# Four pairs of sampled products added by accumulating transfers, and the next image's sums on ScalarE, in a deformable convolution kernel

## The chip, the cores and the metric

One core of a Trainium2 chip runs the whole program. The time is that of the device, in microseconds, from one launch. Each engine runs its own queue in order: TensorE (PE), VectorE (DVE), ScalarE (ACT), GpSimd (POOL) and SyncE (SP). They meet only at semaphores. POOL and SP also issue transfers, which the core's 16 DMA engines carry out; POOL's can add to what lies at their destination.

## What is computed

An image batch (8, 64, 64, 256) goes through two layers, each `x = x + conv(groupnorm(x))`. The change touches only the first, a deformable convolution with 32 groups of 8 channels and 9 taps:

```
xdw    = depthwise3x3(x) + dw_b
om     = xdw @ om_w + om_b          # per group: 9 offsets (x, y), 9 masks
value  = x @ vp_w + vp_b
out[g] = sum over 9 taps of mask * bilinear(value[g], at tap + offset)
x      = x + out @ op_w
```

Group norm needs mean and variance of each group of 8 channels over the 64 x 64 pixels of an image. The second layer is a binarised 3x3 convolution, which the change leaves alone.

## The kernel before

Offsets here stay under one pixel, so the nine taps with bilinear weights fall on a fixed 5 x 5 window of shifts. `layer0` therefore makes 25 weight planes (`wsum`), multiplies the values by each, shifted, and sums the 25 products.

Image n is worked in four steps j = 0 to 3, so 32 steps s = 4n + j in all. In a step 128 partitions are 4 row blocks x 32 groups, with 4 rows x 64 columns = 256 pixels and 8 channels each. A step runs over nine taps k = 0 to 8, and work of neighbouring steps is interleaved:

- For each tap PE makes offsets and mask (`ps_om`, L746), two taps ahead. ACT turns them into hat functions and mask (`hat`, `msk`, L583 to L597). DVE multiplies mask by the hats (`mwy`, L923) and then makes nine products (L937), called P0 to P8 below. The products that start a plane go to `wsum`, the rest to `prod`. Those in `prod` are added to `wsum` by DVE for k = 4, 5, 8 (L965) and by an accumulating transfer of POOL for k = 1, 2, 3, 6, 7 (`SENT_TAPS`, L474); k = 7 takes two transfers. P(k+1) waits until the sum of tap k has landed (L943), since `prod` is used again.
- DVE multiplies shift uv, called M0 to M24, `pv` <- `val` x plane (L984), into one of four buffers, `(j + uv) % 4`, of 128 x 2048 float32 = 1 MiB. It waits for the sum of shift uv - 4 (`add_done`, L981).
- PE adds each product into PSUM by 16 transposing matmuls against the identity (`add`, L791). `SAMPLES_AT` says at which k which shifts are made: M0 to M12 at k = 4 to 8, M13 to M24 at k = 0 to 3 of the next step. PE's order is the same: one shift between the offsets of a tap, the others at the tap's end.
- At k = 4 ACT copies the finished sum into `acc`, PE turns it back (`turn_back`, L759) and ACT keeps `acc_t`; at k = 5, 6 PE projects it. POOL then adds x to `xres` by four accumulating transfers (L464), and DVE takes their statistics (`statistics`, L994) a step later, at k = 0.
- SP loads windows and the rows for the depthwise product. A load is issued when PE has used up what lay there, mostly at k = 0 to 3.

The next image's group norm needs its statistics early. For j = 0 and 1 of each image but the last, POOL loads half of one channel half (128 x 2048) into `acc` once `turn_back` has read it (L457, waiting for "back3" at k = 4), and the other half into `acc_t` once the projection is done. DVE takes `bn_stats` of `acc` at k = 7 (`sums_ahead`, L883) and of `acc_t` at k = 0 of the next step, four instructions each time. At j = 2 DVE aggregates them at k = 0 (`scales_ahead`, L896), PE averages over groups, and the scales are ready at k = 6.

Of the kernel before, what the change touches and what calls it, by code (L numbers as in the profile page):

```python
# [12 lines left out]
P = 128  # L13
H = W = 64
HW = H * W
# [21 lines left out]
SAMPLED = 4  # L37
SENT_TAPS = (1, 2, 3, 6, 7)
# [190 lines left out]
def layer0(nc, x, zeros, w_dram, x2, consts, tables, mv2, reach, NI):  # L229


    with ExitStack() as ctx:
# [26 lines left out]
        bs1 = sb("bs1", [P, CH, HW // 512, 6])  # L259
# [32 lines left out]
        pv_full, add_done, add_out = sem("pv_full"), sem("add_done"), sem("add_out")  # L292
        xres_added, stats2 = sem("xres_added"), sem("stats2")
        gn_kept = sem("gn_kept")
        x_ahead = [sem("x_ahead0"), sem("x_ahead1")]
        sums_made, gx_step = sem("sums_made"), sem("gx_step")
        gx_root = sem("gx_root")
        GX_STEPS = 11
# [54 lines left out]
        with nc.Block() as block:  # L353
# [97 lines left out]
            def _(pool):  # L451
# [24 lines left out]

                for n in range(NI):
                    for j in range(STEPS):
                        for k in SENT_TAPS:
                            if k == 6 and j < CH and n < NI - 1:  # L480
                                load_ahead(n, j, 0, "back3")
                            add_products(n, j, k)
                        if j < CH and n < NI - 1:
                            load_ahead(n, j, 1, "project3")
                        if (n, j) != (0, 0):
                            add_residual(*previous(n, j), unit(n, j, "project3", NI) + 1)

# [13 lines left out]
            def _(act):  # L501
# [98 lines left out]
                def summed(s):  # L600

                    act.wait_ge(add_done, SHIFTS * (s + 1))
# [21 lines left out]
                def keep_mean(n, j, i):  # L624

                    act.wait_ge(bg_full, unit(n, j, f"mean{i}", NI) + 2)
                    nc.scalar.activation(gmean[:, i, :], ps_bg[:, bank(n, j, f"mean{i}", NI), 0:CH], ACT.Copy)\
                        .then_inc(bg_free, 2)

# [20 lines left out]
                def step(n, j, first, last):  # L650
# [8 lines left out]
                    for k in range(TAPS):  # L659
                        if k in MEANS_AT and has_means(n, j, NI):  # L660
                            keep_mean(n, j, MEANS_AT.index(k))
                        if k == ROOT_AT and has_means(n, j, NI):
                            act.wait_ge(gx_step, GX_STEPS * n + 9)
# [26 lines left out]
                        if k == 6 and not last and j1 == 0:  # L690
                            normalise(n1, j1, 1)
                        if k == 8 and more:
# [10 lines left out]
            def _(pe):  # L703
# [72 lines left out]
                def group_mean(n, j, i, src):  # L776


                    pe.wait_ge(gx_step, GX_STEPS * n + (4, 8)[i])
# [4 lines left out]
                def add(s, j, uv):  # L784
                    pe.wait_ge(pv_full, SHIFTS * s + uv + 1)
                    if uv == 0:
                        at_least(pe, add_out, s)
                    for tb in range(TB):
                        for c in range(GC):

                            mm = nc.tensor.matmul(ps_add[:, tb, c, :], pv[:, (j + uv) % PBUF, c, P * tb:P * tb + P],  # L791
                                                  consts["ident"][:, :], start=uv == 0 and c % 4 == 0,
                                                  stop=uv == SHIFTS - 1, is_transpose=True, skip_group_check=True)
# [11 lines left out]
                def step(n, j, first, last):  # L805
# [3 lines left out]
                    def add_next(k, i):  # L809
                        if k < SAMPLED and not first:  # L810
                            add(s - 1, j - 1, SAMPLES_AT[k][i])
                        elif k >= SAMPLED and i < len(SAMPLES_AT[k]):
                            add(s, j, SAMPLES_AT[k][i])
# [4 lines left out]
                    for k in range(TAPS):  # L818
# [9 lines left out]
                        add_next(k, 0)  # L828
# [15 lines left out]
                        add_next(k, 1)  # L844
                        add_next(k, 2)
# [4 lines left out]
                for k in range(SAMPLED):  # L850
                    for uv in SAMPLES_AT[k]:
# [8 lines left out]
            def _(dve):  # L860
# [18 lines left out]
                def sums_ahead(n, j, half):  # L879

                    dve.wait_ge(x_ahead[half], 16 * (CH * n + j + 1))
                    for i in range(HW // 1024):
                        last = nc.vector.bn_stats(bs1[:, j, HW // 1024 * half + i, :], ahead[half][:, 512 * i:512 * i + 512])  # L883
                    last.then_inc(sums_made, 1)

                def scales_ahead(n, j, part):
# [6 lines left out]
                    if part == 0:  # L893

                        for h in range(CH):
                            nc.vector.bn_aggr(mv1[:, h, :], bs1[:, h, :, :]).then_inc(gx_step, 1)  # L896
                        dve.wait_ge(gx_step, GX_STEPS * n + 1 + CH)
                        after(3, nc.vector.tensor_copy(mean1[:, :], mv1[:, :, 0]))
                    elif part == 1:

                        dve.wait_ge(bg_free, unit(n, j, "mean0", NI) + 2)
                        after(4, nc.vector.tensor_tensor(mean1[:, :], mean1[:, :], gm, ALU.subtract))
                        after(5, nc.vector.tensor_tensor(mean1[:, :], mean1[:, :], mean1[:, :], ALU.mult))
                        after(6, nc.vector.tensor_tensor(var1[:, :], mv1[:, :, 1], mean1[:, :], ALU.add))
                        nc.vector.nop().then_inc(gx_step, 1)
                    elif part == 2:
                        dve.wait_ge(bg_free, unit(n, j, "mean1", NI) + 2)
                        after(8, nc.vector.tensor_scalar(var1[:, :], gmean[:, 1, :], EPS, None, ALU.add))
                    else:
# [3 lines left out]
                        after(9, nc.vector.reciprocal(gx[:, 0, :], var1[:, :]))  # L913
                        after(10, nc.vector.scalar_tensor_tensor(out=gx[:, 1, :], in0=gm, scalar=-1.0,
                                                                 in1=gx[:, 0, :], op0=ALU.mult, op1=ALU.mult))

                        after(11, nc.vector.tensor_scalar(tables[:, 0:2, bass.ds((n + 1) * CH, CH)], gx[:, :, :], 1.0, None,
# [50 lines left out]
                def multiply(n, j, uv):  # L968
# [11 lines left out]
                    if not isinstance(s, int) or s > 0 or uv >= PBUF:  # L980
                        dve.wait_ge(add_done, SHIFTS * s + uv - PBUF + 1)  # L981
# [33 lines left out]
                def step(n, j, first, last):  # L1015
# [7 lines left out]
                    for k in range(TAPS):  # L1023
# [13 lines left out]
                        if k == AHEAD_AT and j < CH and has_next(n):  # L1037
                            sums_ahead(n, j, 0)
                        if k == 0 and j in (1, 2) and has_next(n):
                            sums_ahead(n, j - 1, 1)  # L1040
# [834 lines left out]
```

## Time and profile before

| | us |
|---|---|
| median of 3 runs | 3881.9 |
| lowest, highest | 3876.69, 3891.0 |
| profiled execution, its own time | 3880.13 |
| its span, first to last instruction | 3878.3 |
| first layer's 31 step periods, 175.84 to 3368.84 us | 3193.0 |

The profile has a page with busy times of each engine, groups of instructions by source line with the idle time ahead of them and what ended it, the waits, the transfers, and a timeline. A step is recognised by the one `TENSOR_REDUCE` of L1010 at k = 8; the last table line is the distance between the first and the last of the 32. PE and DVE are both above 95% busy in it, while ACT is at 62%. The DMA engines are busy 52% of it, and that load comes in bursts.

### The profile page before, as it was taken

To read this page: it belongs to the slowest core of one execution; us is meant where nothing else is said; L and a number is where in the kernel's file an instruction comes from. 1 tells how busy PE (TensorE), PEld (TensorE's weight loads), DVE (VectorE), ACT (ScalarE), POOL (GpSimd) and SP (SyncE) were. 2 spreads that over 40 slices of the span, in tenths; PEclk is the share of its full clock that TensorE was granted. 3 is DMA by queue.
4 is the path that set the end of the run, shared out by engine and by line. 5 is a ranking of instruction groups with operands and counts; after the bars stand their busy time and mean duration, and the time that the engine had idled before them with its cause. 6 is when DMAs were issued, how large, how long until landed. Compare 5 with 4: busy or idle time off the path is not lost. (4 is left out here: it accounts for less than half of the span.)

```text
span 3878.3 us, 90671 instructions
## 1 busy us (share of the span) xinstructions
PE 3634.4 (94%) x37696; PEld 2370.7 (61%) x37696; DVE 3511.8 (91%) x2757; ACT 2286.1 (59%) x4547; POOL 565.0 (15%) x412
## 2 busy tenths in 40 slices
PE   3799999999999999999999999999999999858998
PEld 1466666666666666666666666666666666623333
DVE  2799999999999999999999999989999999958776
ACT  3665666666556656666666666665566665325554
POOL 0011100111111111111110111111111111104444
PEclk9999999999999999999999999999999999979999
DMA  5454555556554455456545555555545544335563
GB/s 142 109 118 100 116 112 121 111 109 121 131 121 100 96 124 122 101 110 132 129 98 115 117 124 119 109 113 126 117 98 107 105 103 94 60 147 201 214 215 146
DMA packets 319939, 470.35 MB, mean 121 GB/s; under 512 B 37244, under 2 KB 242684, under 8 KB 313736
## 3 DMA queue, kind: packets, MB, share of 16 engines
q0 software_dynamic: 94080, 196.11, 28.2%
q1 hardware_dynamic: 224872, 266.08, 23.0%
q8 instruction: 298, 4.88, 0.5%
q10 hardware_dynamic: 544, 2.10, 0.1%
q14 instruction: 145, 1.19, 0.1%
HBM read 262.53 MB, written 67.41 MB: 85 GB/s over the span
## 5 line engine op out<-in xcount | busy, mean ns | idle before, releaser
L984 DVE TENSOR_TENSOR pv<-val,wsum 128x2048 f32<-128x2048 f32 x800 | 1812.5, 2288 | 7.4 <-PE ps_add L791 7.4
L791 PEld LDWEIGHTS ps_add<-ident,pv 128*128 128x128 f32 x12800 | 1403.0, 142 | 350.0 <-issue 237.2
L791 PE MATMUL ps_add<-ident,pv 128*128 128x128 f32 x12800 | 1529.5, 276 | 65.4 <-DVE pv L984 57.1
L746 PE MATMUL ps_om<-xdw,omw 128*32 128x256 f32 x13824 | 872.0, 385 | 26.9 <-ACT hat L585 26.0
L937 DVE TENSOR_TENSOR prod<-hat,mwy 128x1536 f32<-128x1536 f32 (+1 forms) x384 | 526.5, 1399 | 96.5 <-DMA wsum<-prod 75.5
L474 POOL DMA_DIRECT2D wsum<-prod x192 | 226.0, 1254 | 2598.9 <-DVE wsum L937 2598.9
L583 ACT ACTIVATE hat<-ps_om,omb 128x256 f32<-128x256 f32 x576 | 276.1, 479 | 552.1 <-PE ps_om L746 506.8
L746 PEld LDWEIGHTS ps_om<-xdw,omw 128*32 128x32 f32 x13824 | 391.8, 110 | 328.6 <-issue 95.9
L587 ACT ACTIVATE msk<-ps_om,omb 128x256 f32<-128x256 f32 x288 | 137.1, 476 | 401.6 <-PE ps_om L746 399.4
L923 DVE TENSOR_TENSOR mwy<-hat,msk 128x768 f32<-128x768 f32 x288 | 275.0, 955 | 93.8 <-ACT hat L597 93.8
L718 PE MATMUL ps_bg<-tri,diag 128*32 128x512 f32 x3024 | 347.3, 593 | 0.0
L731 PE MATMUL ps_bg<-win,vpw 128*32 128x256 f32 x5120 | 304.2, 384 | 35.3 <-DMA ident<-in_ident_dram 27.1
L538 ACT ACTIVATE tri<-tri,gn_tri 96x1024 f32<-96x1024 f32 (+1 forms) x376 | 329.9, 951 | 8.7 <-ACT gn_tri L509 4.5
L585 ACT ACTIVATE hat<-ps_om,omb 128x256 f32<-128x256 f32 x576 | 281.4, 489 | 0.0
L584 ACT ACTIVATE hat<-ps_om,nomb 128x256 f32<-128x256 f32 x576 | 276.7, 480 | 0.0
L937 DVE TENSOR_TENSOR wsum<-hat,mwy 128x768 f32<-128x768 f32 (+2 forms) x288 | 257.9, 895 | 2.7 <-DVE pv L984 1.3
L731 PEld LDWEIGHTS ps_bg<-win,vpw 128*32 128x32 f32 x5120 | 167.3, 111 | 149.5 <-DMA ident<-in_ident_dram 27.1
L772 PE MATMUL ps_bg<-acc_t,opw 128*128 128x512 f32 x512 | 238.4, 606 | 1.8 <-ACT acc_t L612 0.7
L965 DVE TENSOR_TENSOR wsum<-wsum,prod 128x1536 f32<-128x1536 f32 x192 | 226.2, 1221 | 0.0
L1688 POOL TENSOR_TENSOR c_x<-c_x,c_res 128x1024 f32<-128x1024 f32 x64 | 170.4, 2666 | 340.5 <-ACT c_res L1572 340.5
L1641 PE MATMUL ps_p<-c_over,c_kw 128*128 128x512 bf16 x768 | 189.0, 396 | 18.8 <-ACT c_res L1566 18.8
L718 PEld LDWEIGHTS ps_bg<-tri,diag 128*32 128x32 f32 x3024 | 98.9, 111 | 176.0 <-issue 155.4
(120 smaller groups left out, 2607.8 us busy)
## 6 DMA issues: line engine op xcount, KB each, us to landing
wsum<-prod POOLq DMA_DIRECT2D x160, 768.0 KB, 7.0
tri<-in_x_dram SPq DMA_DIRECT2D x725, 128.0 KB, 2.9
win<-in_x_dram SPq DMA_DIRECT2D x148, 256.0 KB, 3.5
x<-xres SPq DMA_DIRECT2D x128, 256.0 KB, 5.2
xres<-in_x_dram POOLq DMA_DIRECT2D x124, 256.0 KB, 8.7
out_dram<-c_x SPq DMA_DIRECT2D x31, 1024.0 KB, 4.7
c_x<-x SPq DMA_DIRECT2D x30, 1024.0 KB, 5.4
c_box<-box_d SPq DMA_DIRECT2D x16, 1024.0 KB, 7.1
```

The lines of the kernel that those rows point to most:

```text
L538: last = nc.scalar.activation(v, v, ACT.Identity, bias=gn_tri[0:KROWS, j % 2, 2 * c + 1, h:h + 1], scale=gn_tri[0:KROWS, j % 2, 2 * c, h:h ...
L583: nc.scalar.activation(hat[:, par, a, 1, :], d, ACT.Abs, bias=b).then_inc(abs_done, 1)
L584: nc.scalar.activation(hat[:, par, a, 0, :], d, ACT.Relu, bias=nb, scale=-1.0)
L585: nc.scalar.activation(hat[:, par, a, 2, :], d, ACT.Relu, bias=b).then_inc(om_free, 1)
L718: mm = nc.tensor.matmul(out[:, :, :, o0:o1], diag[:, h, c, kx, :], src, start=kx == 1, stop=kx == 2)
L731: mm = nc.tensor.matmul(ps_bg[G * q:G * q + G, par, ci * TOK:(ci + 1) * TOK], vpw[:, h, 2 * cp + ci, :], win[:, h, q, :, :], start=h == 0, ...
L746: mm = nc.tensor.matmul(ps_om[G * q:G * q + G, (par + i) % 2, 0:TOK], omw[:, h, comp, :], xdw[:, j % 2, h, q, :], start=h == 0, stop=h == ...
L772: mm = nc.tensor.matmul(ps_bg[:, par, :], opw[:, h, P * oh:P * oh + P], acc_t[:, h, 512 * tb:512 * tb + 512], start=h == 0, stop=h == CH - 1)
L791: mm = nc.tensor.matmul(ps_add[:, tb, c, :], pv[:, (j + uv) % PBUF, c, P * tb:P * tb + P], consts["ident"][:, :], start=uv == 0 and c % 4 ...
L923: nc.vector.tensor_tensor(mwy[:, :, :], hat[:, par, 1, :, :], msk[:, par, :].unsqueeze(1).to_broadcast([P, 3, TOK]), ALU.mult)\
L937: return nc.vector.tensor_tensor(dst, hat[:, par, 0, c:d, :].unsqueeze(1).to_broadcast(shape), mwy[:, a:b, :].unsqueeze(2).to_broadcast(sh ...
L984: nc.vector.tensor_tensor(pv[:, (j + uv) % PBUF, :, :].rearrange("p c (r w) -> p c r w", w=W), val[:, :, SR * j + u:SR * j + u + SR, v:v + ...
```

## The change

Two things change.

**Pairs.** For (target <- source) 1 <- 0, 3 <- 2, 12 <- 11 and 15 <- 14, POOL issues a transfer that adds the source's product buffer, 1 MiB, into the target's (`add_pair`). PE adds the target alone, so 21 shifts. PE's wait for a target is for the transfer (`pair_added`). DVE's wait before it writes a buffer that held a source is for the transfer as well. PE's order becomes `ADDS_AT`.

**Sums.** `sums_ahead` moves from DVE to ACT. At k = 7, and at k = 0 of the next step, ACT subtracts a pivot (the half's first value) from the 2048 values in place and accumulates the sum, then squares them and accumulates again. `scales_ahead` makes mean and variance out of those sums by five small instructions in place of two `bn_aggr` and a copy. DVE's wait for `sums_made` at k = 0 of j = 2 stays.

```diff
+PAIRED = {1: 0, 3: 2, 12: 11, 15: 14}
+ADDS_AT = [(13, 12), (16, 15, 17, 18), (19, 20, 21), (22, 23, 24), (), (1,), (4, 3, 5, 6), (7, 8, 9), (10,)]
...
+                def add_pair(n, j, uv):
+
+                    s = STEPS * n + j
+                    pool.wait_ge(pv_full, SHIFTS * s + uv + 1)
+                    at_least(pool, pair_added, 16 * (len(PAIRS) * s + PAIRS.index(uv)))
+                    nc.gpsimd.dma_start(pv[:, (j + uv) % PBUF, :, :], pv[:, (j + PAIRED[uv]) % PBUF, :, :], accum_op=ALU.add)\
+                        .then_inc(pair_added, 16)
+
                 for n in range(NI):
                     for j in range(STEPS):
+                        if (n, j) != (0, 0):
+                            add_pair(*previous(n, j), 15)
                         for k in SENT_TAPS:
-                            if k == 6 and j < CH and n < NI - 1:
-                                load_ahead(n, j, 0, "back3")
+                            if k == 6:
+                                if j < CH and n < NI - 1:
+                                    load_ahead(n, j, 0, "back3")
+                                add_pair(n, j, 1)
+                                add_pair(n, j, 3)
                             add_products(n, j, k)
                         if j < CH and n < NI - 1:
                             load_ahead(n, j, 1, "project3")
                         if (n, j) != (0, 0):
                             add_residual(*previous(n, j), unit(n, j, "project3", NI) + 1)
+                        add_pair(n, j, 12)
+                add_pair(NI - 1, STEPS - 1, 15)
...
+                def sums_ahead(n, j, half):
+
+                    act.wait_ge(x_ahead[half], 16 * (CH * n + j + 1))
+                    v, i = ahead[half], 3 * (CH * n + j)
+                    if half == 0:
+                        nc.scalar.activation(pivot[:, j:j + 1], v[:, 0:1], ACT.Copy, scale=-1.0).then_inc(centred, 1)
+                        act.wait_ge(centred, i + 1)
+                    nc.scalar.activation(v, v, ACT.Identity, bias=pivot[:, j:j + 1],
+                                         accum_out=x_sums[:, half, j, 0:1]).then_inc(centred, 1)
+                    act.wait_ge(centred, i + 2 + half)
+                    nc.scalar.activation(v, v, ACT.Square, accum_out=x_sums[:, half, j, 1:2]).then_inc(sums_made, 1)
...
                 def add(s, j, uv):
-                    pe.wait_ge(pv_full, SHIFTS * s + uv + 1)
-                    if uv == 0:
+                    if uv in PAIRED:
+                        pe.wait_ge(pair_added, 16 * (len(PAIRS) * s + PAIRS.index(uv) + 1))
+                    else:
+                        pe.wait_ge(pv_full, SHIFTS * s + uv + 1)
+                    if uv == ADDED[0]:
                         at_least(pe, add_out, s)
...
-                    if not isinstance(s, int) or s > 0 or uv >= PBUF:
-                        dve.wait_ge(add_done, SHIFTS * s + uv - PBUF + 1)
+                    used, in_step = (uv - PBUF, s) if uv >= PBUF else (uv - PBUF + SHIFTS, s - 1)
+                    if used in PAIRED.values():
+                        dve.wait_ge(pair_added, 16 * (len(PAIRS) * in_step + list(PAIRED.values()).index(used) + 1))
+                    elif not isinstance(s, int) or in_step >= 0:
+                        dve.wait_ge(add_done, ADDS * in_step + ADDED.index(used) + 1)
```

POOL's queue, from the first product transfers of a step with j = 1 to the next step's, before: `wsum<-prod` are the transfers of L474 for k = 1, 2, 3, 6, 7, `xres` the residual.

```order
L474 DMA wsum<-prod 128x3x512 [waits wsum_added,prod_done] x2
L474 DMA wsum<-prod 128x2x768 [waits wsum_added,prod_done]
L457 DMA acc<-in_x_dram 128x2048 [waits bg_full]
L474 DMA wsum<-prod 128x2x768 [waits wsum_added,prod_done] x2
L474 DMA wsum<-prod 128x512
L457 DMA acc_t<-in_x_dram 128x2048 [waits bg_full]
L464 DMA xres<-in_x_dram 128x2x256 [waits bg_free]
L464 DMA xres<-in_x_dram 128x2x256 x3
```

Now, from the same place on, with the pairs 1, 3 and 12, 15 as `pv<-pv`:

```order
L481 DMA wsum<-prod 128x3x512 [waits wsum_added,prod_done] x2
L481 DMA wsum<-prod 128x2x768 [waits wsum_added,prod_done]
L464 DMA acc<-in_x_dram 128x2048 [waits bg_full]
L489 DMA pv<-pv 128x2048 [waits pair_added,pv_full] x2
L481 DMA wsum<-prod 128x2x768 [waits wsum_added,prod_done] x2
L481 DMA wsum<-prod 128x512
L464 DMA acc_t<-in_x_dram 128x2048 [waits bg_full]
L471 DMA xres<-in_x_dram 128x2x256 [waits bg_free]
L471 DMA xres<-in_x_dram 128x2x256 x3
L489 DMA pv<-pv 128x2048 [waits pair_added,pv_full] x2
```

Pairs 1 and 3 stand ahead of the product transfer of k = 6, pair 12 behind the residual and pair 15 ahead of the product transfer of k = 1, each with a wait for the pair before it.

DVE's queue at k = 6 of a step with j = 1, before: the end of P6, then M4, the mask, M5 and M6.

```order
L937 TENSOR_TENSOR wsum<-hat,mwy 128x768
L981 REGISTER_ALU [waits wsum_added]
L984 TENSOR_TENSOR pv<-val,wsum 128x2048 [waits add_done]
L922 REGISTER_ALU [waits prod_done]
L923 TENSOR_TENSOR mwy<-hat,msk 128x768 [waits hat_full]
L981 REGISTER_ALU [waits wsum_added]
L984 TENSOR_TENSOR pv<-val,wsum 128x2048 [waits add_done]
L981 REGISTER_ALU [waits wadd_done]
L984 TENSOR_TENSOR pv<-val,wsum 128x2048 [waits add_done]
```

Now:

```order
L974 TENSOR_TENSOR wsum<-hat,mwy 128x768
L1019 ISA [waits wsum_added]
L1024 TENSOR_TENSOR pv<-val,wsum 128x2048 [waits pair_added]
L959 REGISTER_ALU [waits prod_done]
L960 TENSOR_TENSOR mwy<-hat,msk 128x768 [waits hat_full]
L1021 ISA [waits wsum_added]
L1024 TENSOR_TENSOR pv<-val,wsum 128x2048 [waits add_done]
L1019 ISA [waits wadd_done]
L1024 TENSOR_TENSOR pv<-val,wsum 128x2048 [waits pair_added]
```

Nothing is moved here; M4 and M6 wait for the transfers of pairs 1 and 3 (`pair_added`) where they waited for PE.

ACT's queue at k = 0 and 1 of a step with j = 2, before: the end of the hats, the depthwise result, the group mean, the next hats.

```order
L597 ACTIVATE hat<-hat 128x2x256 [waits w0_done]
L555 ACTIVATE xdw<-ps_bg,dwb 128x512 [waits bg_full]
L627 ACTIVATE gmean<-ps_bg 128x2 [waits bg_full]
L583 ACTIVATE hat<-ps_om,omb 128x256 [waits om_full,prod_done]
L584 ACTIVATE hat<-ps_om,nomb 128x256
```

Now:

```order
L619 ACTIVATE hat<-hat 128x2x256 [waits w0_done]
L577 ACTIVATE xdw<-ps_bg,dwb 128x512 [waits bg_full]
L659 ACTIVATE acc_t,x_sums<-acc_t,pivot 128x2048 [waits x_ahead1]
L662 ACTIVATE acc_t,x_sums<-acc_t 128x2048 [waits centred]
L649 ACTIVATE gmean<-ps_bg 128x2 [waits bg_full]
L605 ACTIVATE hat<-ps_om,omb 128x256 [waits om_full,prod_done]
```

Two activations over 128 x 2048 stand between the depthwise result and the group mean.

## Rows read from the trace of the kernel before

**Rows 1.** Groups by line: shapes, count | busy us, mean ns | idle before, releasers.

```profile
L984 DVE TENSOR_TENSOR pv<-val,wsum 128x2048 f32<-128x2048 f32 x800 | 1812.5, 2288 | 7.4 <-PE ps_add L791 7.4
...
L791 PE MATMUL ps_add<-ident,pv 128*128 128x128 f32 x12800 | 1529.5, 276 | 65.4 <-DVE pv L984 57.1 <-ACT acc L604 7.8
...
L604 ACT ACTIVATE acc<-ps_add 128x1024 f32<-128x1024 f32 x64 | 62.1, 1022 | 67.3 <-PE ps_add L791 67.3
...
L883 DVE BATCH_NORM_STATS2 bs<-acc 128x6 f32<-128x512 f32 x56 | 34.6, 684 | 0.0
...
L883 DVE BATCH_NORM_STATS2 bs<-acc_t 128x6 f32<-128x512 f32 x56 | 34.5, 681 | 0.0
```

**Rows 2.** Window: us; PE, PEld, DVE, ACT, POOL busy; clock, DMA share, GB/s.

```profile
175.84:3368.84 3193.00, 3104.74 (x34384) 2127.15 (x34380) 3051.86 (x2274) 1968.04 (x4098) 386.01 (x336) 1.00 0.52 112
```

**Rows 3.** Waits of DVE in that window: us, times, longest us.

```profile
DVE prod L937 <- DMA wsum<-prod: 64.7, 62, 2.2
DVE mwy L923 <- ACT hat L597: 40.8, 32, 3.8
DVE prod L937 <- issue: 16.3, 12, 3.2
```

**Rows 4.** Three short windows, columns as in the long one above.

```profile
1032.00:1033.00 1.00, 0.19 (x1) 0.19 (x2) 1.00 (x2) 0.97 (x3) 0.14 (x1) 0.90 0.32 57
1033.00:1036.00 3.00, 3.00 (x15) 3.00 (x15) 3.00 (x3) 0.00 (x0) 0.00 (x0) 0.50 1.11 193
...
1103.00:1105.00 2.00, 2.00 (x26) 1.66 (x28) 2.00 (x4) 1.13 (x4) 0.11 (x1) 1.00 1.04 368
```

**Rows 5.** DMA issues, 1030.5 to 1040 us: KB each, us to landing.

```profile
wsum<-prod POOLq DMA_DIRECT2D x1, 768.0 KB, 6.5
```

**Rows 6.** DMA issues of the whole span, page part 6.

```profile
acc<-in_x_dram POOLq DMA_DIRECT2D x14, 1024.0 KB, 5.3
```

**Rows 7.** Timeline of POOL, start us, us.

```profile
1030.85 1.28 POOL L474 DMA_DIRECT2D wsum<-prod  x1 [30.89 <-DVE wsum L937]
...
1075.58 0.59 POOL L457 DMA_DIRECT2D acc<-in_x_dram  x1 [20.27 <-PE ps_bg L759]
```

**Rows 8.** Timeline of DVE, k = 8 to k = 2, two steps.

```profile
1013.24 2.56 DVE L937 TENSOR_TENSOR wsum<-hat,mwy 128x2304 f32<-128x2304 f32 x1
...
1018.79 4.49 DVE L984 TENSOR_TENSOR pv<-val,wsum 128x2048 f32<-128x2048 f32 x2
...
1027.94 1.75 DVE L937 TENSOR_TENSOR prod<-hat,mwy 128x1536 f32<-128x1536 f32 x1
...
1037.94 0.60 DVE L1001 BATCH_NORM_AGGREGATE mv_now<-bs 128x2 f32<-128x48 f32 x2
...
1127.06 2.47 DVE L883 BATCH_NORM_STATS2 bs<-acc_t 128x6 f32<-128x512 f32 x4
...
1208.60 2.36 DVE L937 TENSOR_TENSOR prod<-hat,mwy 128x1536 f32<-128x1536 f32 x2 [2.14 <-DMA wsum<-prod]
```

**Rows 9.** Timeline of DVE, k = 5 to k = 7 of one step.

```profile
1071.72 2.36 DVE L937 TENSOR_TENSOR prod<-hat,mwy 128x1536 f32<-128x1536 f32 x2
...
1081.87 1.76 DVE L937 TENSOR_TENSOR prod<-hat,mwy 128x1536 f32<-128x1536 f32 x1
...
1084.40 2.29 DVE L984 TENSOR_TENSOR pv<-val,wsum 128x2048 f32<-128x2048 f32 x1
...
1087.47 4.50 DVE L984 TENSOR_TENSOR pv<-val,wsum 128x2048 f32<-128x2048 f32 x2
...
1091.88 2.37 DVE L937 TENSOR_TENSOR prod<-hat,mwy 128x1536 f32<-128x1536 f32 x2
```

**Rows 10.** Timeline of ACT, k = 0 and 1 of step j = 2.

```profile
1128.77 0.69 ACT L555 ACTIVATE xdw<-ps_bg,dwb 128x512 f32<-128x512 f32 x1 [0.71 <-PE ps_bg L718]
1133.38 0.17 ACT L627 ACTIVATE gmean<-ps_bg 128x2 f32<-128x2 f32 x1 [3.91 <-PE ps_bg L781]
```

**Rows 11.** Timeline of SyncE's queue, loads for the depthwise product.

```profile
1025.37 17.61 SPq L381 DMA_DIRECT2D tri<-in_x_dram  x12
```

## What is predicted, and from what

> **What bounds the kernel now.** I read the groups by line first, for who costs what; then the busy times of the stretch from the end of step 0 to the end of step 31, 3193.0 us; then what VectorE waits for in it; and last the timelines of single steps, because the change acts there.
>
> In that stretch VectorE is busy 3051.9 us and TensorE 3104.7 [rows 2]. Neither alone sets the pace. VectorE is idle 141.1 us, made up of 64.7 + 16.3 = 81 us at the start of a P, which is the transfer of the tap before (the profile names no releaser for the second figure, but it stands at the same instruction), 40.8 us for ACT's hats, 7.4 us for PE's sums and small rests [rows 1, 3]. The hats are late where PE has fallen behind; they and the 7.4 us are what a lighter PE can give back. The 81 us are transfers, and no engine's load changes them. So a lighter PE is worth at most 48 us, and what VectorE sheds comes on top.
>
> **What is taken away.** PE: four shifts a step. One is 1529.5 / 12800 x 16 = 1.91 us [rows 1], so 7.6 us a step and 237 us over 31 steps. PE then has 2868 us of work in 3193. It is no bound any more, and of the 237 us only the 48 above can reach the end. VectorE: the 112 `bn_stats`, 34.6 + 34.5 = 69.1 us [rows 1]. The five small instructions for mean and variance take the place of two aggregations and a copy, 7 times; I set that even. Together 48 + 69 = **117 us to be gained**, if nothing new is waited for.
>
> **What a pair costs as a transfer.** No row shows one, so I build it from the nearest: the product transfer of 768 KB, also accumulating, between the same memories and from the same queue. Issued at 1030.85 [rows 7], it moves data from about 1032.7 on at 193 GB/s, with the 16 engines full (share 1.11) [rows 4], and lands 6.5 us after its issue [rows 5]. That is 1.7 us to start, 0.786 MB / 193 GB/s = 4.1 us to move and 0.7 us to land. POOL wakes 0.4 us after DVE has finished. A pair is 1.049 MB: 0.4 + 1.7 + 5.4 + 0.7 = **8.2 us** from DVE's last write to the release. The other end is the plain load of 1 MiB, 5.3 us [rows 6] at 368 GB/s [rows 4]. I take 193, since an accumulating transfer has to read two operands for one written and the row nearest in kind shows about half the plain rate.
>
> The Trainium skill ("DMA: Bandwidth & Descriptors", Anatomy of one DMA — SWDGE (gpsimd) path) fits such a transfer as 2.0 us plus bytes / 436e3. By it a pair would take 4.4 us, an estimate from that page, and 768 KB 3.8 us. The trace doesn't agree for accumulating transfers: it has 6.5 us for 768 KB [rows 5]. What a fast pair would give is a rival below.
>
> **Where the pairs meet VectorE.** All times are from the example step, as distances.
>
> Pair 12. M12 ends at 1013.24 and M15, which writes over source 11, would begin at 1018.79 + 2.20 = 1020.99 [rows 8]: 7.75 us for an 8.2 us transfer. Late by 0.45 us alone, by up to 3 if SyncE's window load falls on it. I take 0.7 x 31 = **22 us**.
>
> Pair 15. It is issued as M15 ends, and P1 follows after the statistics alone, so P1 ends 5.0 us after M15. The pair moves from 2.1 to 7.5, the product transfer of k = 1 behind it in the queue to 11.6, and it lands at 12.3. P2 wants it at 5.0 + 7.5 = 12.5: P1 to P2 is 10.0 us [rows 8], 2.5 of it P1. Nothing is lost alone, but SyncE issues twelve loads of 128 KB from 1025.37 on [rows 11], half of them onto the pair; their 0.8 MB at the mixed rate cost about 3 us, and the slack is 0.2. I take 2.5 us, of which some 0.5 is in the 81 us already: 2.0 x 24 = **48 us** for all steps but the seven below (bounds 0 and 4 us each).
>
> Pairs 1 and 3 and the product transfer of k = 6. From the end of M1 (1071.72 = 0) [rows 9]: pair 1 lands at 8.2. M3 ends at 10.15, pair 3 is issued at 10.55 and moves from 12.25 to 17.65. P6 ends at 12.7; its product transfer is behind pair 3, moves from 17.65 to 21.75 and lands at 22.45. P7 would begin at 20.16 [rows 9]. Late by 2.3 us, where it is on time now; 17 steps, 39 us.
> In the 14 steps with j < 2 the 1 MiB load of `acc` goes out first. Its issue is at 1075.58 = 3.9 [rows 7]; with PE one shift lighter ahead of it I put 3.0. It moves from 4.7 to 7.55, pair 1 to 12.95 and lands at 13.65. Pair 3 waits for that landing before it is issued, moves from 15.45 to 20.85, and the product transfer to 24.95, landing at 25.65. Late by 5.5 us, 77 us. Together **116 us** (bounds: 2.3 in all, 71; 7 and 3.5, 158). What stands behind these waits on VectorE is P7, M7 to M9 and with them PE's next shifts.
>
> **Where the sums go.** ACT does 1024 elements in 1.02 us [rows 1], so two passes over 2048 are about 4.1 us, 28 times, 115 us on an engine that is busy 1968 of 3193 [rows 2]. Between the depthwise result, which ends at 1129.46, and the group mean ACT sits idle 3.91 us now [rows 10]; that cover is used up. But VectorE waits for `sums_made` at k = 0 of j = 2. M15 ends there at 1127.06 [rows 8] and ACT would be done at 1129.46 + 4.1 = 1133.6: 6.5 us of a new wait, 7 times, **46 us**. Statistics and P1 are queued behind it. Pair 15 lands under this wait, which is why P2 costs nothing in these steps. If ACT came to it sooner, it would be some 4 us (30 us).
>
> At k = 7 the sums have been covering something too. P8 waits for two product transfers; in a step without sums it waits 2.14 us [rows 8], and this kind of wait is 1.6 to 2.1 us in each of the seven steps that show it. With the sums away the steps j = 0 and 1 show it, and with PE no longer late the steps j = 3 too: 1.9 x 24 = **46 us**.
>
> **The sum.** New waits 22 + 48 + 116 + 46 + 46 = 278 us, against 117 gained: 161 us slower. From the profiled execution's 3880.1 us (span 3878.3; the median of the runs is 3881.9) that gives 4041 us. With the bounds of the terms, 14 + 0 + 71 + 30 + 46 = 161 at the low end, it would be 3924; at the high end 93 + 96 + 158 + 60 + 60 = 467, or 4230.
>
> **The rivals.**
> *Fast pairs.* The pairs move at the plain 368 GB/s. Then pair 12 lands in time, pair 3 moves from 12.25 to 15.1, and the product transfer lands at 19.9, before P7's 20.16. What is left of the new waits is 46 + 46 and some 10, or 102, against 117: 3865 us, no difference. For it speaks that a pair lies in 8 KB rows, as the plain load does, and the product transfer in shorter ones; against it the two operands read, which the length of a row doesn't change.
> *Fast pairs and hidden sums.* The same, and ACT gets to its sums before VectorE waits for them, since the lighter PE feeds it sooner: 56 against 117, or 3819 us, faster. This is the case the page's 4.4 us would lead to. Its turning point is where a pair takes less than 7.75 us from write to release, and the sums are done by 1127 in the example.
> *Half of it.* Rates as I have them, but the loads keep out of the way and the sums wait is short: 3900 to 3930.
> *TensorE's clock.* After 2.13 us of idleness PE was granted 0.90 and then 0.50 of its speed for three microseconds, the 1.2 GHz level [rows 4], and 16 matmuls of L791 took 3.6 us there where they take 1.9 otherwise. A PE that pauses at five or six places a step meets that each time. It has 325 us of slack, but if two such delays of 1.6 us a step reach VectorE through the hats, that is 100 us more: 4140 us.
>
> **How the numbers follow.** The forecast with its own spread, 3930 to 4120, 62 in 100. TensorE's clock or more collisions, above 4120, 13. Half of it, 6. Fast pairs alone, 8. Fast pairs and hidden sums, or something else that leaves the gain, 11. A measurement of this kernel can tell 0.5%, about 19 us. Below 3862 I put 0.13, between 3862 and 3901 0.09, and above 0.78. The range leaves out the fast cases and the far end: 3865 to 4160.
>
> **What would show it.** Right: VectorE's waits at the start of P7 grow from almost none to over 2 us a step, twice that where j < 2; the wait ahead of M15 is short but in each step; one long wait for ACT per image, at k = 0 of j = 2; PE's busy time is down by 245 us with much more idle time; the stretch of 31 steps is about 3354 us. The pairs take 7.8 us from issue to landing. Wrong: pairs that land in 5 to 6 us (fast pairs); no wait ahead of the statistics of j = 2; hats that VectorE waits for, which would mean that PE or ACT is the bound.

## The result and the profile after

| | before | after |
|---|---|---|
| median of 4 runs, us | 3883.2 | 4106.7 |
| lowest, highest | 3876.7, 3891.0 | 4097.3, 4113.8 |
| ratio, with its 95% interval | | 1.0573 [1.0544, 1.0602] |
| span of the profiled execution | 3878.3 | 4095.5 |
| first layer's 31 step periods | 3193.0 | 3401.8 |

The change costs 223.5 us. Forecast were 161 (4041 us; the range was 3865 to 4160). The first layer's 31 periods hold 208.8 of it. Their window row answers to [rows 2]: PE, PEld, DVE, ACT, POOL busy, granted clock, DMA share, GB/s.

```profile
177.38:3579.22 3401.84, 2984.67 (x32412) 1985.44 (x32404) 2992.83 (x2180) 2076.11 (x4221) 496.69 (x460) 0.95 0.69 143
```

PE has 120 us less to do, VectorE 59 us less, ACT 108 more. Nobody is at the limit now, and the stretch is still longer: the time is in waits. VectorE's, in the same stretch (us, times, longest), against [rows 3]:

```profile
DVE prod L974 <- DMA wsum<-prod: 182.8, 93, 4.2
DVE pv L1024 <- DMA pv<-pv: 87.2, 52, 3.9
DVE bs L1034 <- ACT acc_t L662: 46.7, 7, 7.8
DVE prod L974 <- issue: 42.7, 19, 4.8
DVE pv L1024 <- PE ps_add L832: 37.5, 25, 3.3
```

The wait for hats has gone from the list. Waits ahead of a P, for product transfers, rose from 81 to 225.5 us (first and fourth line), and three more kinds are new or larger. By line (count | busy, mean ns | idle before), against [rows 1], and the transfers (KB, us from issue to landing), against [rows 5, 6]:

```profile
L1024 DVE TENSOR_TENSOR pv<-val,wsum 128x2048 f32<-128x2048 f32 x800 | 1813.2, 2286 | 131.0 <-DMA pv<-pv 91.5
L832 PE MATMUL ps_add<-ident,pv 128*128 128x128 f32 x10752 | 1352.2, 285 | 298.3 <-DVE pv L1024 247.9
```

```profile
pv<-pv POOLq DMA_DIRECT2D x128, 1024.0 KB, 8.2
wsum<-prod POOLq DMA_DIRECT2D x160, 768.0 KB, 7.7
```

VectorE's multiplies cost what they did. PE, whose sums had 65 us of idle time ahead of them, has 298. A pair takes 8.2 us from issue to landing, forecast 7.8. Here is the step with j = 1 that answers to [rows 7, 9], POOL first:

```profile
1132.66 0.58 POOL L464 DMA_DIRECT2D acc<-in_x_dram  x1 [19.59 <-PE ps_bg L797]
1133.23 0.90 POOL L489 DMA_DIRECT2D pv<-pv  x1
1144.69 0.85 POOL L489 DMA_DIRECT2D pv<-pv  x1 [10.56 <-DMA pv<-pv]
1145.23 1.53 POOL L481 DMA_DIRECT2D wsum<-prod  x1
```

```profile
1129.11 2.35 DVE L974 TENSOR_TENSOR prod<-hat,mwy 128x1536 f32<-128x1536 f32 x2
...
1137.06 2.29 DVE L1024 TENSOR_TENSOR pv<-val,wsum 128x2048 f32<-128x2048 f32 x1
...
1144.18 2.29 DVE L1024 TENSOR_TENSOR pv<-val,wsum 128x2048 f32<-128x2048 f32 x1 [2.30 <-DMA pv<-pv]
...
1153.41 2.29 DVE L1024 TENSOR_TENSOR pv<-val,wsum 128x2048 f32<-128x2048 f32 x1 [3.86 <-DMA pv<-pv]
...
1157.16 2.36 DVE L974 TENSOR_TENSOR prod<-hat,mwy 128x1536 f32<-128x1536 f32 x2 [1.46 <-DMA wsum<-prod]
```

M1 ends at 1129.11, where P5 (first line) begins. The load of `acc` goes 3.55 us later (forecast 3.0), pair 1 right behind it. M3 (second line) ends at 1139.35, but POOL, idle for 10.56 us in all, issues pair 3 only at 1144.69, when pair 1 has landed: 5.3 us late. The product transfer stands behind pair 3. So M4 waits for pair 1, M6 for pair 3 and P7 for the product: three waits where [rows 9] has none. P7 begins 28.05 us after M1, forecast 25.65, before 20.16.

### The profile page after: what moved, and what is told of

It is laid out like the page before. It is cut to its first block and busy times, and to the rows that moved or that the text cites. A ratio compares the mean times of both kernels' runs of the same rounds, so it can differ in the third digit from the quotient of the medians.

```text
span 4095.5 us, 86912 instructions
## 1 busy us (share of the span) xinstructions
PE 3507.0 (86%) x35648; PEld 2226.4 (54%) x35648; DVE 3450.4 (84%) x2659; ACT 2397.6 (59%) x4673; POOL 679.2 (17%) x540
## 5 line engine op out<-in xcount | busy, mean ns | idle before, releaser
L832 PE MATMUL ps_add<-ident,pv 128*128 128x128 f32 x10752 | 1352.2, 285 | 298.3 <-DVE pv L1024 247.9
L832 PEld LDWEIGHTS ps_add<-ident,pv 128*128 128x128 f32 x10752 | 1244.8, 147 | 553.0 <-DVE pv L1024 339.3
L784 PE MATMUL ps_om<-xdw,omw 128*32 128x256 f32 x13824 | 901.4, 395 | 90.6 <-ACT hat L607 89.7
L784 PEld LDWEIGHTS ps_om<-xdw,omw 128*32 128x32 f32 x13824 | 403.0, 112 | 433.5 <-ACT hat L607 126.2
L489 POOL DMA_DIRECT2D pv<-pv x128 | 112.4, 878 | 1441.4 <-DVE pv L1024 1289.7
L960 DVE TENSOR_TENSOR mwy<-hat,msk 128x768 f32<-128x768 f32 x288 | 274.2, 952 | 51.9 <-ACT hat L619 51.9
```

What stands on the lines that cost most here:

```text
L784: mm = nc.tensor.matmul(ps_om[G * q:G * q + G, (par + i) % 2, 0:TOK], omw[:, h, comp, :], xdw[:, j % 2, h, q, :], start=h == 0, stop=h == ...
L960: nc.vector.tensor_tensor(mwy[:, :, :], hat[:, par, 1, :, :], msk[:, par, :].unsqueeze(1).to_broadcast([P, 3, TOK]), ALU.mult)\
```

## The waits, place by place

VectorE's order in a step is fixed, so each wait in its timeline can be put to the instruction ahead of which it stands. The sums below are over the 31 periods, worked out so from the timelines (us; a dot is under 2). The last line but one is the sum of all waits. The kernels E1 to E12 are those of the next section.

| wait ahead of | before | after | E1 | E2 | E3 | E4 | E5 | E6 |
|---|---|---|---|---|---|---|---|---|
| mask (hats) | 40.9 | . | . | 52.6 | . | . | . | 27.1 |
| M15 | 2.0 | 20.6 | 14.7 | 2.0 | . | 18.1 | . | 27.5 |
| P2 | 10.5 | 69.4 | 58.7 | 15.1 | 2.7 | 68.6 | 3.5 | 37.5 |
| P3, P4 | 51.9 | 28.2 | 34.2 | 48.2 | 51.7 | 29.5 | 51.9 | 49.6 |
| M4, M6 | . | 65.9 | 77.4 | . | . | 3.1 | 65.2 | . |
| P7 | 4.9 | 73.0 | 76.1 | 4.0 | 4.2 | 80.0 | 78.0 | 6.9 |
| M5, M7 | . | 19.1 | 17.6 | . | 79.7 | 11.8 | 18.3 | . |
| P8 | 15.9 | 57.1 | 36.6 | 17.3 | 9.7 | 59.8 | 60.9 | 36.0 |
| statistics (ACT) | . | 46.6 | . | 61.3 | 49.3 | 47.1 | 36.3 | 45.8 |
| M16, M17, M19 | . | 18.5 | 12.4 | . | 23.4 | 14.6 | . | 49.5 |
| all | 135.0 | 402.2 | 330.6 | 211.2 | 223.6 | 337.4 | 317.7 | 287.6 |
| stretch | 3193.0 | 3401.8 | 3394.7 | 3207.2 | 3218.3 | 3335.8 | 3314.5 | 3285.2 |

From before to after the waits grow by 267.2 us and VectorE's busy time falls by 59.0, which is the stretch's 208.

## The experiments

Each diff is against the kernel after, cut where it shows `...`. All ratios are against the kernel before, run beside it on the same chip.

**E1, the pairs alone.** `sums_ahead` and its means are VectorE's again, as before.

```diff
...
+                    for i in range(HW // 1024):
+                        last = nc.vector.bn_stats(bs1[:, j, HW // 1024 * half + i, :], ahead[half][:, 512 * i:512 * i + 512])
...
```

> The four pairs as in the changed kernel, the sums back on VectorE as before. My theory puts the loss on the pairs' transfers in VectorE's way: bn_stats give VectorE 69 us of work back, but the 47 us wait for ACT at k = 0 of j = 2 goes, and the bn_stats at k = 7 cover the wait for the product transfers ahead of P8 again in 14 steps (about 30 us). So 4085 to 4115 us, about the changed kernel's 4107. The rival that the sums on ACT are what costs expects 3880 to 3920.

**E2, the sums alone.**

```diff
-PAIRED = {1: 0, 3: 2, 12: 11, 15: 14}
-ADDS_AT = [(13, 12), (16, 15, 17, 18), (19, 20, 21), (22, 23, 24), (), (1,), (4, 3, 5, 6), (7, 8, 9), (10,)]
+PAIRED = {}
+ADDS_AT = [(13, 14, 15), (16, 17, 18), (19, 20, 21), (22, 23, 24), (0, 1), (2, 3), (4, 5, 6), (7, 8, 9), (10, 11, 12)]
...
```

> The sums on ACT, no pairs: TensorE adds 25 shifts. My theory: VectorE loses 69 us of work and gains a wait of about 45 us for ACT and some 27 us ahead of P8, and TensorE still paces the steps with j = 2 and 3, so 3870 to 3900 us. The rival that the sums on ACT carry the loss expects 4050 or more. It also gives the size of the wait for ACT when TensorE is not lightened: 6.5 us in seven places.

Measured: E1 4094.6 us, 1.0554 [1.0535, 1.0573]; E2 3895.7 us, 1.0041 [1.0026, 1.0055]. The first rows of VectorE's waits in E1, then in E2:

```profile
DVE prod L963 <- DMA wsum<-prod: 158.2, 91, 4.8
DVE pv L1013 <- DMA pv<-pv: 92.0, 45, 5.5
```

```profile
DVE prod L970 <- DMA wsum<-prod: 63.3, 69, 2.0
DVE bs L1030 <- ACT acc_t L658: 61.3, 7, 9.5
```

The pairs are 5.5% and the sums 0.4%. The two add up within the intervals: over the kernel before, run beside them (3879.5 us), 215 + 16 us against 224. So the 69 us of `bn_stats` were not worth 69: in E2 61.3 came back as one long wait for ACT per image, and 12 more as later hats.

**E3, an eighth of each pair.** The transfers add one of the 8 channels.

```diff
-                    nc.gpsimd.dma_start(pv[:, (j + uv) % PBUF, :, :], pv[:, (j + PAIRED[uv]) % PBUF, :, :], accum_op=ALU.add)\
+                    nc.gpsimd.dma_start(pv[:, (j + uv) % PBUF, 0:1, :], pv[:, (j + PAIRED[uv]) % PBUF, 0:1, :], accum_op=ALU.add)\
```

> The changed kernel with each pair's transfer adding only one of the eight channels (128 KB in place of 1 MiB); the other seven are left out, all issues and waits stay. If the bytes are the cost, the waits ahead of M4, M6, M15 and the additional ones ahead of P2 and P7, some 205 us together, go: 3885 to 3925 us. If the waits and POOL's issues themselves are the cost (a fixed price per transfer), it stays above 4050.

Measured: 3911.7 us, 1.0086 [1.0065, 1.0107]. The pairs' row of its transfers, and two of VectorE's waits:

```profile
pv<-pv POOLq DMA_DIRECT2D x128, 128.0 KB, 2.8
```

```profile
DVE pv L1024 <- PE ps_add L832: 103.1, 53, 3.7
DVE prod L974 <- DMA wsum<-prod: 52.5, 56, 2.6
```

All semaphores, the order of the queues and PE's lighter load are those of after; only the bytes are fewer, and a row of a transfer is 1 KB where it was 8. 195 of the 223 us go. The waits at M4, M6, M15, P2 and P7 are gone with them, so it is the length of the transfers that costs, not their number or their issue. Between the two sizes 5.4 us are spent on 0.918 MB, or 170 GB/s, near the 193 that [rows 4] have for a product transfer and less than half of the plain load's 368. The 5.4 us are also what tells rates from start-up costs: a 128 KB transfer still takes 2.8. But even this kernel, which leaves 7/8 of the pairs' bytes out, doesn't beat the one before. 61.5 us of its waits stand ahead of M7, for PE's sum of shift 3, which `ADDS_AT` has behind the sum of 4 at k = 6.

**E4, the load last.** POOL issues the load of `acc` behind pairs 1, 3 and the product transfer.

```diff
                             if k == 6:
-                                if j < CH and n < NI - 1:
-                                    load_ahead(n, j, 0, "back3")
                                 add_pair(n, j, 1)
                                 add_pair(n, j, 3)
                             add_products(n, j, k)
+                            if k == 6 and j < CH and n < NI - 1:
+                                load_ahead(n, j, 0, "back3")
```

> The changed kernel with the 1 MiB load of acc issued behind pairs 1 and 3 and the product transfer of k = 6, not ahead of them. My theory: in the 14 steps with j < 2 the waits ahead of M4, M6 and P7 fall from 7.2 us a step to the 2 to 2.5 us of j = 2, 14 x 5 = 70 us, so about 4035 us. The rival that the DMA engines' total load is what counts expects the wait to turn up elsewhere (P8) and 4090 to 4110.

Measured: 4037.2 us, 1.0405 [1.0387, 1.0424]. Of VectorE's waits:

```profile
DVE prod L974 <- DMA wsum<-prod: 192.7, 94, 4.8
DVE pv L1024 <- DMA pv<-pv: 22.1, 29, 1.7
```

A line moved within one queue is worth 70 us. The wait at M4 goes altogether and that at M6 but for 3.1; P7's stays, now 80.0, some 2.6 us in each of 31 steps, which is the 2.3 that I had worked out for a step without the load.

**E5 and E6, half of the pairs.** E5 keeps 1 and 3, E6 keeps 12 and 15; the rest of `ADDS_AT` is as in E2.

```diff
+PAIRED = {1: 0, 3: 2}      # E5
...
+PAIRED = {12: 11, 15: 14}  # E6
...
```

> The changed kernel with pairs 1 and 3 only; 12 and 15 are added by TensorE again. Counted from the sums-only run (3896 us): the waits at k = 4 to 7 as in the changed kernel, 153 us, less the 53 us wait for hats, plus 35 us ahead of P8 that a late TensorE hides: about 4030 us. If the cost were the DMA engines' load as a whole, half the pairs would cost half of 211 us: about 4000 us, and the waits at k = 4 to 7 would be halved.

> The changed kernel with pairs 12 and 15 only. From the sums-only run: M15 20 us, P2 54 us more, sums 12 and 15 late on TensorE for M16 and M19 18 us, P8 35 us, less 53 us of hats and 14 us of the wait for ACT: about 3955 us. The part for P2 comes from pair 15 alone. With the load as a whole as the cause it would be about 4000, as the run with pairs 1 and 3.

Measured: E5 3999.0 us, 1.0295 [1.0274, 1.0315]; E6 3975.3 us, 1.0238 [1.0221, 1.0255]. Pair waits in E5, then in E6:

```profile
DVE pv L1022 <- DMA pv<-pv: 65.2, 31, 5.1
```

```profile
DVE pv L1022 <- PE ps_add L830: 53.9, 30, 5.6
DVE pv L1022 <- DMA pv<-pv: 27.5, 26, 2.4
```

E5 came out 31 us under my figure, E6 20 over. E5's time is the one that the rival, the load of the DMA engines as a whole, had for it (about 4000). But that rival wanted the waits of k = 4 to 7 halved, and they are not smaller than in after (161.5 against 158.0), so pairs 1 and 3 cost there what they cost. My figure, counted up from E2, was too high because I had left two waits as E2 has them: the statistics, 36.3 us in place of 61.3, and P2, 3.5 in place of 15.1. In E6 the surprise is M16, 45.9 us, a wait for PE: M16 writes over product 12, whose sum `ADDS_AT` places at the end of k = 0, where before had it at k = 8. P2, which comes behind M16, waits 37.5 us and not the 69 that I had expected of pair 15 alone. Taken singly the two halves cost 103 and 80 us over E2, 183 in all, against 211 together.

**E7, the two pairs best placed.** Pairs that VectorE gives most time: 1 and, at k = 0, 13 <- 12; the load last, the sums on VectorE.

```diff
+PAIRED = {1: 0, 13: 12}
+ADDS_AT = [(13, 14, 15), (16, 17, 18), (19, 20, 21), (22, 23, 24), (), (2, 1, 3), (4, 5, 6), (7, 8, 9), (10, 11)]
...
```

> Only pairs that VectorE's order leaves room for: 1 <- 0 (12.7 us from the end of M1 to M4) and 13 <- 12 (10.2 us from the end of M13 to M16), the load of acc behind the product transfer of k = 6, sums on VectorE. A transfer of 8.2 us fits into both and no product transfer queues behind it. My theory: no new wait beyond some 13 us ahead of P8, and the 48 us that VectorE waits for a late TensorE go: 3840 to 3865 us, faster than before. If any accumulating transfer of 1 MiB costs VectorE time wherever it stands, 3920 or more.

Measured: 3933.5 us, 1.014 [1.012, 1.016]. Of VectorE's waits:

```profile
DVE pv L1011 <- PE ps_add L813: 76.7, 24, 6.4
DVE mwy L947 <- ACT hat L616: 11.4, 18, 0.9
```

The transfers are off the path: P7 5.7, P2 7.1, and no wait for a pair. In their place stands PE, 64.7 us ahead of M5, 59.4 of it in the steps j = 0 and 3. There the sum of shift 1 comes late behind the value products of k = 5. Expected was a gain of 20 to 40 us; that was wrong.

**E8, sums in time with eighth pairs.** As E3, and PE takes shift 3 at k = 5, ahead of M7's need.

```diff
-ADDS_AT = [(13, 12), (16, 15, 17, 18), (19, 20, 21), (22, 23, 24), (), (1,), (4, 3, 5, 6), (7, 8, 9), (10,)]
+ADDS_AT = [(13, 12), (16, 15, 17, 18), (19, 20, 21), (22, 23, 24), (), (1, 3), (4, 5, 6), (7, 8, 9), (10,)]
```

> The run with eighth pairs (one of eight channels added, the rest left out) and TensorE's sum of shift 3 at the end of k = 5, not behind the projection at k = 6. That run's VectorE waits 61.5 us for that sum ahead of M7; if the order of the sums is the reason, 55 to 65 us go: about 3850 us. If TensorE's load is the reason, it stays at 3900 to 3915.

**E9, the sums sooner.** As E2, with ACT's second half at the end of k = 8 and not at k = 0.

```diff
-                        if k == 0 and j in (1, 2) and has_next(n):
-                            sums_ahead(n, j - 1, 1)
...
+                        if k == 8 and j < CH and has_next(n):
+                            sums_ahead(n, j, 1)
```

> No pairs; ACT makes the second half's sums at k = 8, behind the tri normalisation, and not at k = 0 of the next step. The sums-only run (3896 us) waits 61 us for them on VectorE ahead of the statistics of j = 2. If that wait is all that stands against the move, 25 to 50 us of it come back as time, the rest as waits for a TensorE that has only 88 us of idle time: 3850 to 3875 us. If ACT's 4.1 us at k = 8 delay hats and depthwise inputs as much, it stays at 3890 to 3900.

Measured: E8 3910.2 us, 1.0079 [1.0062, 1.0096], where some 3850 was expected; E9 3921.3 us, 1.0103 [1.0087, 1.0118], where 3850 to 3875 was. Waits in E8, then in E9:

```profile
DVE pv L1024 <- PE ps_add L832: 56.5, 24, 4.7
DVE prod L974 <- DMA wsum<-prod: 90.2, 68, 3.2
```

```profile
DVE mwy L956 <- ACT hat L615: 108.1, 73, 3.8
DVE bs L1030 <- ACT acc_t L658: 27.8, 7, 4.0
```

Both did what they were made for, and both lost it again at once. In E8 the 61.5 us ahead of M7 are gone, and P8 waits 57.0 where it waited 9.7: with M7 in time, P8 comes up before the transfers of k = 7 have landed. In E9 the wait for ACT fell from 61.3 to 27.8 us and the hats' rose from 52.6 to 108.1. 42.6 us of that rise stand in the steps j = 1, right behind the first of the moved sums, so I put it to ACT's four microseconds ahead of those hats. A wait's total is no price: behind it stands the next one.

**E10 to E12, one pair alone.** E10 has only 13 <- 12, sums on VectorE; at k = 0 PE then has its sums of 13, 14 and 15 all at the tap's end. E11 is E7 with the sum of 1 ahead of the values at k = 5. E12 is E10 with 14 first, in the gap between the offset products, where before had 13.

```diff
+PAIRED = {13: 12}                # E10, E12
+ADDS_AT = [(14, 13, 15), ...     # E12; E10 has (13, 14, 15)
...
```

> One pair, 13 <- 12, sums on VectorE: the transfer has 10.2 us and nothing queues behind it. TensorE is 59 us lighter. Of the 41 us that VectorE waits for hats 30 or so go, 12 come ahead of M17 and 10 ahead of P8: 3865 to 3880 us, at best a little faster. If the transfer itself cost time here, 3900 or more.

> The run with pairs 1 and 13 (3933 us), with TensorE's sum of shift 1 moved from the end of k = 5 to ahead of the values and the projection. That run's VectorE waits 65 us ahead of M5 for that sum. If the miss lay in the late sum, 50 to 65 us go: 3870 to 3885 us. If it lay in the two transfers, it stays at 3920 to 3935.

> The run with the single pair 13 <- 12 (3955 us), with one change of order: TensorE adds shift 14 between the offset products at k = 0, where that run has nothing and its TensorE stands 5.9 us for ACT's hats, and the pair's sum after it. If that hole in TensorE's order is what made the single pair slower, the waits for hats fall from 107 us to about 40 and the time to 3865 to 3890 us. If the transfer itself disturbs ACT or TensorE, it stays above 3940.

Measured: E10 3955.4 us, 1.0194 [1.0181, 1.0208]; E11 3951.7 us, 1.0183 [1.0168, 1.0199]; E12 3920.8 us, 1.0107 [1.009, 1.0124]. All three were expected at 3865 to 3890. The hats' rows of E10, E11 and E12:

```profile
DVE mwy L946 <- ACT hat L615: 107.3, 61, 4.3
```

```profile
DVE mwy L951 <- ACT hat L616: 89.4, 52, 4.4
```

```profile
DVE mwy L946 <- ACT hat L615: 63.3, 40, 3.8
```

PE at the start of an image (j = 0, k = 0) in E10:

```profile
936.09 1.93 PE L764 MATMUL ps_om<-xdw,omw 128*32 128x256 f32 x16 [5.88 <-ACT hat L603]
937.80 3.99 PE L736 MATMUL ps_bg<-tri,diag 128*32 128x512 f32 x24
941.72 5.46 PE L812 MATMUL ps_add<-ident,pv 128*128 128x128 f32 x48
```

PE has nothing to do for 5.88 us: the sum of 13 isn't in the gap any more, as it waits for its pair, and the hats are late. Then PE runs slowly: 24 matmuls take 3.99 us at a mean granted clock of 0.68, against 2.73 us at 1.00 for the same group later in E12 (last row below). Three sums in a row follow, 5.46 us, and the next offsets behind them. A sum of another shift in the gap (E12) is worth 35 us, and the wait for hats at j = 0 falls from 58.9 to 31.2:

```profile
929.64 1.15 PE L764 MATMUL ps_om<-xdw,omw 128*32 128x256 f32 x16 [4.14 <-ACT hat L603]
930.55 4.41 PE L736 MATMUL ps_bg<-tri,diag 128*32 128x512 f32 x24
...
943.18 2.73 PE L736 MATMUL ps_bg<-tri,diag 128*32 128x512 f32 x24
```

The second row is the same slowing in E12, at a mean clock of 0.62 behind 4.14 us of idle time. E7 leaves the same gap of PE empty at k = 0 and waits 11.4 us for hats; with its wait ahead of M5 taken away (64.7 us, none in E11) the hats' wait is 89.4 us, and E11 is slower than E7.

The swap doesn't bring the kernel back to the one before, though it differs from it by one pair. Of the 63.3 us for hats 31.2 are at j = 0. There ACT itself starts late, and the timeline names nothing that it waits for:

```profile
928.39 0.47 ACT L601 ACTIVATE hat<-ps_om,omb 128x256 f32<-128x256 f32 x1 [2.61 <-issue]
```

E10 has 2.45 us of it at the same place; before goes on without a pause there. In that idle time the trace has one packet of an instruction queue, between 926 and 927 us, beside a window load that fills the 16 engines (E12's transfers in that microsecond: packets, MB, share of 16 engines):

```profile
q1 hardware_dynamic: 372, 0.36, 103.9%
q14 instruction: 1, 0.01, 1.9%
```

In E10 that packet comes between 933 and 934 us, and ACT resumes at 934.84. Before has it while ACT is still busy with the previous group. So ACT may be waiting for its next instructions here. No run tests that, and it stays open.

## Why the prediction was right, and where it was not

The sign, the mechanism and the places were right. The size was 62.5 us short (223.5 against 161; 208.8 in the stretch and 14.7 outside it). Term by term, in us of new waits; the measured column is after less before in the table of places:

| term | forecast | measured |
|---|---|---|
| pair 12, at M15 | 22 | 18.6 |
| pair 15, at P2 | 48 | 58.9 |
| pairs 1, 3 and their load, at k = 4 to 7 | 116 | 153.1 |
| sums, at the statistics | 46 | 46.6 |
| P8 uncovered | 46 | 41.2 |
| hats and PE given back | -48 | -46.3 |
| `bn_stats` gone | -69 | -59.0 |
| PE late at M16, M19 | none | 18.5 |
| P3 and P4 covered by the wait at P2 | none | -23.7 |
| sum | 161 | 208 |

**The transfer's price** came out near, partly by luck: the median pair takes 8.2 us from issue to landing against 7.8, which rested on 193 GB/s out of [rows 4]. That such a transfer is slow is shown directly where pair 3 of the example moves and nothing else does (after, 1146.5 to 1151 us), in packets of 8 KB:

```profile
DMA packets 111, 0.91 MB, mean 202 GB/s; under 512 B 0, under 2 KB 0, under 8 KB 0
q0 software_dynamic: 111, 0.91, 102.3%
```

But the price isn't one number. By pair the medians in after are 8.5 us (pair 1), 7.0 (3), 8.3 (12) and 8.4 (15), and E7, where no load and no other pair stands ahead of one, has for its 64

```profile
pv<-pv POOLq DMA_DIRECT2D x64, 1024.0 KB, 7.4
```

So a pair with nothing beside it is quicker than I had it, and what stands beside it brings the median up: in the example pair 1, behind the load, took 10.9 us. A product transfer, which I had put at 6.5 us from one row, has a median of 7.7 (7.0 before). By the Trainium skill ("DMA: Bandwidth & Descriptors", Anatomy of one DMA — SWDGE (gpsimd) path) a pair would take 4.4 us, an estimate; the trace doesn't agree, the quickest of the 128 pairs of after took 6.9. With it the rivals of fast pairs are out: the median pair 12 doesn't make the 7.75 us that M15 gives.

**The step that was mis-sized** is the one on pairs 1 and 3 and the product transfer of k = 6. It put 2.3 us to 17 steps and 5.5 to 14, 116 us, and the waits at M4 to M7 and P7 measured 153.1, near its own upper bound of 158. One slip is small: the stretch has 13 steps with the load and 18 without, which at the same prices is 113 us. In the 13 the waits come to 7.4 us and not 5.5. The example shows why: `acc` was issued 0.55 us later than I had it, pair 1 landed 15.1 us after M1 (forecast 13.65), pair 3 24.3 (21.55) and the product transfer 28.05 (25.65). The wait at P7 alone isn't twice as long there, as I had written it would be: it is 2.4 us, and the rest of the lateness stands at M4 and M6. At j = 2 the waits are 2.0 us, and the 2.3 held. At j = 3 they come to 5.1, of which 2.1 are M5 and M7 waiting for something that the step didn't have: PE. (P7's share there is 3.0; what makes it longer than at j = 2 stays open.) The rows of PE, then VectorE's:

```profile
1359.13 3.64 PE L769 MATMUL ps_bg<-win,vpw 128*32 128x256 f32 x64
...
1366.66 1.91 PE L832 MATMUL ps_add<-ident,pv 128*128 128x128 f32 x16
```

```profile
1368.61 4.49 DVE L1024 TENSOR_TENSOR pv<-val,wsum 128x2048 f32<-128x2048 f32 x2 [2.26 <-PE ps_add L832]
```

The sum of 1 is PE's last work at k = 5, behind 64 value products. M5 takes its buffer and waits. That and M16, M19 (18.5 us) are the second miss: I wrote that PE "is no bound any more", which holds for its load but not for its order. `ADDS_AT` moved sums to where the pairs let them be, and they came late for the buffers that wait for them. E3 (61.5 us at M7), E6 (45.9 at M16) and E7 (64.7 at M5) each show such a wait, and E10 what it costs to leave PE's gap empty. What these waits are worth as time is less sure: E8 and E11 took one away each and gained nothing.

**What was over-counted.** P3 and P4 wait 23.7 us less than before. I had kept them whole. Perhaps a long wait at P2 lets the transfers of the following taps catch up: after, E1 and E4 have 59 to 69 us at P2 and 28 to 34 at P3 and P4, and E2, E3 and E5 at most 15 and at least 48. E6, with 37.5 and 49.6, doesn't fit, so this isn't shown. That these 23.7 us nearly cancel the 18.5 of PE is luck. `bn_stats` gave 59 and not 69: 2.5 us of the 69.1 lie ahead of the stretch. In the records two consecutive instructions of VectorE overlap by 0.09 us, and a wait between them ends that, so the 76 more waits of after, the shortest included, account for about 7.

**Outside the stretch** 14.7 us remain. The span holds 8.4 of them, before the first and behind the last step end, and I did not place them; the rest is that the profiled execution was the fastest of the four.

**The clock** rival had its condition met, not its price. PE was granted 1.00 on average before [rows 2] and 0.95 in after, down to the 1.2 GHz level behind its pauses. Here is one: 16 matmuls of a sum after 5.92 us without work, and the window of two microseconds in which they begin, with the clock at 0.50:

```profile
1076.14 3.68 PE L832 MATMUL ps_add<-ident,pv 128*128 128x128 f32 x16 [5.92 <-DVE pv L1024]
...
1076.00:1078.00 2.00, 1.86 (x9) 1.86 (x10) 2.00 (x3) 0.58 (x2) 0.00 (x0) 0.50 1.04 217
```

A sum's matmul takes 285 ns on average where it took 276, and PE's busy time fell by 127 us over the program rather than 245. But VectorE waits for hats, by which it was to reach it, nowhere in after. It shows in E10 and E12, by the slow groups above; what these cost VectorE was not told apart from the rest.

**Half of it** and **the sums hidden** are refuted: the ACT wait was there in its full size, ACT's two passes took 2.00 and 1.91 us, and VectorE's statistics began 5.72 us late in the example:

```profile
1196.72 1.91 ACT L662 ACTIVATE acc_t<-acc_t 128x2048 f32<-128x2048 f32 x1
...
1198.85 2.47 DVE L1034 BATCH_NORM_STATS2 bs<-xres 128x6 f32<-128x512 f32 x4 [5.72 <-ACT acc_t L662]
```

## What to carry to other kernels

Work taken from an engine that is not waited for buys only the waits that it causes, here 46 us for the 237 forecast; before it is moved to a transfer, set the transfer's whole time from write to release beside the time after which its buffer is written again, and count everything behind it in the same queue. A unit of work that stands in a gap of its engine is free there; to leave that gap empty cost 35 us (E10 against E12), though the load was the same. A wait that is taken away is worth what it lasts only if nothing stands ready behind it: three edits that removed 34 to 65 us of one wait (E8, E9, E11) gained nothing.

## What was not expected of the hardware

- An accumulating transfer between buffers on the chip moves some 190 to 200 GB/s with the 16 engines full, about half of a plain load's 368, and rows of 8 KB hardly help (202 GB/s for a pair, 193 for a product transfer): 7.4 to 8.2 us for 1 MiB, 2.8 us for 128 KB.
- PE's granted clock falls behind single pauses in the midst of the work: after idle times of 4.14 and 5.88 us (E12, E10) it was 0.62 and 0.68 on average while groups of 24 matmuls took 4.41 and 3.99 us instead of 2.73.
- At the start of an image ACT pauses for 2.61 us in E12 with no releaser in the trace. An instruction packet in that time suggests a cause, which no run tested.
- A fifth product buffer, which would have given the pairs a longer way, was not tried.
